# Expert matrices w1 and w3 loaded per slot tile in four chunks instead of kept in SBUF

## The reference

```python
def _L0_ffn_ref(x, gate_w, w1, w2, w3):          # 8 experts, top 2, DIM 256, HIDDEN 1024
    xt = x.reshape(-1, orig_shape[-1])
    scores = xt @ gate_w.T
    top_vals, top_idx = jax.lax.top_k(scores, TOP_K)
    top_w = jax.nn.softmax(top_vals, axis=-1)
    combine = jnp.einsum('tke,tk->te', jax.nn.one_hot(top_idx, NUM_EXPERTS, dtype=xt.dtype), top_w)
    h = jax.nn.silu(jnp.einsum('td,ehd->eth', xt, w1)) * jnp.einsum('td,ehd->eth', xt, w3)
    ye = jnp.einsum('eth,edh->etd', h, w2)
    y = jnp.einsum('te,etd->td', combine, ye)
    return y.reshape(orig_shape)
x = x + _L0_ffn_ref(_layernorm(x, axis=-1), L0_ffn_gate_w, L0_ffn_w1, L0_ffn_w2, L0_ffn_w3)
```

## Time and profile before

| | before |
|---|---|
| median of three runs | 954.2 us (951.09 to 955.96) |
| the profiled execution's own time | 948.78 us |
| its span | 947.0 us |
| mean granted TensorE clock | 0.915 of full speed |
| PE busy | 823.2 us (87%) |
| DVE busy | 630.4 us (67%) |
| ACT busy | 541.6 us (57%) |
| bytes moved by DMA | 115.83 MB |

### The profile page before, as it was taken

The page is one execution under the profiler, slowest core; times in us unless marked ns, Lnnn a source line. Parts: engine busy times, 40 slices in busy tenths (PEclk is TensorE's granted clock), DMA queues, the critical chain, the costliest instruction groups (busy, mean ns, idle before and its releaser), DMA issues.

```text
span 947.0 us, 24051 instructions
## 1 busy us (share of the span) xinstructions
PE 823.2 (87%) x9192; PEld 715.3 (76%) x9192; DVE 630.4 (67%) x941; ACT 541.6 (57%) x846; POOL 231.4 (24%) x133
## 2 busy tenths in 40 slices
PE   4888879989989998999558369999999999999994
PEld 3555558878888887888458358888888888888884
DVE  3343333636454463646334839999999999999993
ACT  2433336525443352535113129899898999898892
POOL 2244400000000000000000003455554555454542
PEclk8899989979998999989855559999999999999998
DMA  9899940000000000000807213545454545454542
GB/s 358 294 384 373 380 200 2 2 2 2 2 2 2 2 2 3 2 3 3 354 12 257 90 55 111 150 127 144 133 144 133 148 129 144 133 144 133 146 125 62
DMA packets 34661, 115.83 MB, mean 122 GB/s; under 512 B 4289, under 2 KB 15490, under 8 KB 29474
## 3 DMA queue, kind: packets, MB, share of 16 engines
q1 hardware_dynamic: 27010, 104.35, 31.4%
q0 software_dynamic: 7584, 10.49, 6.2%
HBM read 105.26 MB, written 9.57 MB: 121 GB/s over the span
## 4 chain that ended last, share of the span: by engine, by line
PE 78%; DMA 8%; DVE 6%; issue 5%; ACT 1%; SPq 1%; POOLq 0%; DVEq 0%; ACTq 0%
PE ps L428 20%; PE ps L429 19%; PE ps L430 19%; DMA ctx_t<-in_ctxT 6%; PE ps L731 3%; PE ps L614 3%; PE ps L594 2%; PE ps L602 2%; PE ps L683 1%; PE ps L668 1%; PE ps L485 1%; PE ps L507 1%; PE ps L661 1%; PE ps L694 1%; DVE den L1109 1%
## 5 line engine op out<-in xcount | busy, mean ns | idle before, releaser
L1187 DVE TENSOR_TENSOR w_lo<-w,w_hi 128x1024 fp32r<-128x1024 f32 x156 | 194.6, 1286 | 0.4 <-issue 0.4
L403 POOL DMA_INDIRECT xs_sb<-xn_d,slot_row x39 | 68.4, 1753 | 507.1 <-DVE slot_row L1307 429.9
L906 ACT ACTIVATE w_hi<-w 128x1024 fp32r x156 | 161.3, 1062 | 7.3 <-DVE tile_e L1268 7.3
L414 POOL DMA_INDIRECT out_x<-y_sb,slot_row x39 | 119.9, 3075 | 120.8 <-ACT y_sb L938 120.8
L428 PE MATMUL ps<-w_hi,xh 128*128 128x512 f32 x312 | 126.6, 406 | 1.3 <-DVE xl L1330 1.3
L430 PE MATMUL ps<-w_hi,xl 128*128 128x512 f32 x312 | 122.4, 392 | 0.0
L429 PE MATMUL ps<-w_lo,xh 128*128 128x512 f32 x312 | 122.1, 391 | 0.0
L428 PE MATMUL ps<-xT_hi,wa_hi 128*128 128x256 f32 x384 | 114.1, 297 | 2.9 <-DVE xT_lo L1085 1.5
L429 PE MATMUL ps<-xT_lo,wa_hi 128*128 128x256 f32 x384 | 110.3, 287 | 0.3 <-issue 0.3
L430 PE MATMUL ps<-xT_hi,wa_lo 128*128 128x256 f32 x384 | 110.1, 287 | 0.0
L917 ACT ACTIVATE w_hi<-w_sb 128x1024 fp32r<-128x1024 f32 x78 | 82.6, 1062 | 33.0 <-DMA w_sb<-in_w 24.6
(11 more groups left out here) (180 smaller groups left out, 1720.8 us busy)
## 6 DMA issues: line engine op xcount, KB each, us to landing
w_sb<-in_w SPq DMA_DIRECT2D x78, 512.0 KB, 4.7
ctx_t<-in_ctxT SPq DMA_DIRECT2D x16, 1028.0 KB, 7.7
ctx_n<-in_ctxN SPq DMA_DIRECT2D x16, 1024.0 KB
w<-in_w SPq DMA_DIRECT2D x8, 2048.0 KB, 11.9
stage<-in_w_a SPq DMA_DIRECT2D x16, 256.0 KB, 5.6
x_all<-in_x SPq DMA_DIRECT2D x4, 512.0 KB, 6.5
out_x<-x_all SPq DMA_DIRECT2D x1, 2048.0 KB, 13.1
xn_d<-xn SPq DMA_DIRECT2D x4, 512.0 KB, 3.9
```

What stands on the lines that cost most here:

```text
L403: pool.indirect_dma_start(xs_sb[:, :], None, xn_d, bass.IndirectOffsetOnAxis(slot_row[:, t:t + 1], 0)).then_inc(f_xs, 16)
L414: pool.indirect_dma_start(out, bass.IndirectOffsetOnAxis(slot_row[:, t:t + 1], 0), y_sb[:, :], None, compute_op=ALU.add).then_inc(f_st, 16)
L906: act.activation(w_hi[:, c, :].rearrange("p (c n) -> p c n", c=DC), w13[:, bass.ds(e, 1), c % 2, :, c // 2 * 512:(c // 2 + 1) * 512].rearr ...
L1187: dve.tensor_tensor(w_lo[:, c, :].rearrange("p (c n) -> p c n", c=DC), w13[:, bass.ds(e, 1), c % 2, :, c // 2 * 512:(c // 2 + 1) * 512].re ...
```

## The change

w13 and its loads disappear. A single buffer w13_sb of four chunks takes their place, and SP loads the four chunks of a tile's expert for every slot tile, with load_w13 standing before load_w2 in SP's loop. Chunk c of tile t waits until up_lo(t-1, c) has read the one before. up_hi waits for its chunk's semaphore f_w13[c], and ACT and DVE no longer read the expert's index. The host lays w13 out so that each chunk is contiguous within a partition's row.

```diff
-    w13 = nc.alloc_sbuf_tensor_at("w13", [P, E, 2, DC, HID], F32, offset=W13_AT)
+    w13_sb = nc.alloc_sbuf_tensor_at("w13_sb", [P, 4, PC], F32, offset=LATE_AT + EXP_BYTES)
-    l_w13 = sem("l_w13")
+    f_w13 = [sem(f"f_w13_{c}") for c in range(4)]
@@ SP
-        def load_expert(e):
-            sp.dma_start(w13[:, e, :, :, :].rearrange("p w c h -> p (w c h)"), a["w13"][e, :, :]).then_inc(l_w13, 16)
-
-        for e in range(EARLY):
-            load_expert(e)
-        sp.wait_ge(a_v, 4 * NT // 2)
-        for e in range(E // 2, E):
-            load_expert(e)
-        sp.wait_ge(a_num, NT // 2)
-        sp.wait_ge(a_y, NT // 2)
-        for e in range(EARLY + 1, E // 2):
-            load_expert(e)
-
         sp.wait_ge(a_x2, NT // 2)
...
         sp.wait_ge(g_keep, 16 * XQ)
-        sp.wait_ge(g_tr, NT)
-        load_expert(EARLY)
-
+
+        def load_w13(t):
+            e = sp.value_load(tile_e[0:1, bass.ds(t, 1)], min_val=0, max_val=E - 1)
+            for c in range(4):
+                wait(sp, f_ulo, 4 * (t - 1) + c + 1)
+                sp.dma_start(w13_sb[:, c, :], a["w13"][bass.ds(e, 1), :, c * PC:(c + 1) * PC].rearrange("e p n -> (e p) n")).then_inc(f_w13[c], 16)
...
+        sp.wait_ge(r_map, 1)
+        sp.wait_ge(a_y, NT // 2)
+        load_w13(0)
         sp.wait_ge(r_done, 1)
         load_w2(0)
         with sp.Fori(1, SLOT_TILES) as t:
+            load_w13(t)
             load_w2(t)
@@ ACT
-        def up_hi(t, cs, e):
+        def up_hi(t, cs):
             if not valid(t, SLOT_TILES):
                 return
             for c in cs:
+                wait(act, f_w13[c], 16 * (t + 1))
                 wait(act, f_up, 4 * (t - 1) + c + 1)
-                act.activation(w_hi[:, c, :].rearrange("p (c n) -> p c n", c=DC),
-                               w13[:, bass.ds(e, 1), c % 2, :, c // 2 * 512:(c // 2 + 1) * 512].rearrange("p a c n -> p (a c) n"),
-                               ACT.Copy).then_inc(f_uhi, 1)
+                act.activation(w_hi[:, c, :], w13_sb[:, c, :], ACT.Copy).then_inc(f_uhi, 1)
...
         act.wait_ge(r_map, 1)
-        act.wait_ge(l_w13, 16 * E)
-        up_hi(0, range(4), expert(0))
+        up_hi(0, range(4))
@@ DVE
-                dve.tensor_tensor(w_lo[:, c, :].rearrange("p (c n) -> p c n", c=DC),
-                                  w13[:, bass.ds(e, 1), c % 2, :, c // 2 * 512:(c // 2 + 1) * 512].rearrange("p a c n -> p (a c) n"),
-                                  w_hi[:, c, :].bitcast(F32).rearrange("p (c n) -> p c n", c=DC), ALU.subtract).then_inc(f_ulo, 1)
+                dve.tensor_tensor(w_lo[:, c, :], w13_sb[:, c, :], w_hi[:, c, :].bitcast(F32), ALU.subtract).then_inc(f_ulo, 1)
@@ host
-        "w13": np.stack([w1, w3], axis=1).reshape(E, 2, HID, DC, P).transpose(0, 4, 1, 3, 2).reshape(E, P, 2 * DC * HID),
+        "w13": np.stack([w1, w3], axis=1).reshape(E, 2, 2, HID // 2, DC, P).transpose(0, 5, 2, 1, 4, 3).reshape(E, P, 2 * DC * HID),
```

More of the change, by code:

```diff
@@ L944, in h_hi @@
             act.activation(hh[:, :, :], ps[:, 4:6, :].rearrange("p a (c d) -> p (a c) d", c=4), ACT.Copy).then_inc(f_hh, 1)
-        def expert(t):
-            return act.value_load(tile_e[0:1, bass.ds(t, 1)], min_val=0, max_val=E - 1) if valid(t, SLOT_TILES) else None
         def fstep(t):
-            e = expert(t + 1)
             silu(t, 0)
-            up_hi(t + 1, (0, 1), e)
+            up_hi(t + 1, (0, 1))
             silu(t, 1)
-            up_hi(t + 1, (2,), e)
+            up_hi(t + 1, (2,))
             x_hi(t + 1)
-            up_hi(t + 1, (3,), e)
+            up_hi(t + 1, (3,))
             down_hi(t)
@@ L1179, in _, with up_lo @@
             astep(r, r % 2)
-        def up_lo(t, cs, e):
+        def up_lo(t, cs):
             if not valid(t, SLOT_TILES):
@@ L1186, in up_lo @@
                 wait(dve, f_uhi, 4 * t + c + 1)
-                dve.tensor_tensor(w_lo[:, c, :].rearrange("p (c n) -> p c n", c=DC),
-                                  w13[:, bass.ds(e, 1), c % 2, :, c // 2 * 512:(c // 2 + 1) * 512].rearrange("p a c n -> p (a c) n"),
-                                  w_hi[:, c, :].bitcast(F32).rearrange("p (c n) -> p c n", c=DC), ALU.subtract).then_inc(f_ulo, 1)
-        def expert(t):
-            return dve.value_load(tile_e[0:1, bass.ds(t, 1)], min_val=0, max_val=E - 1) if valid(t, SLOT_TILES) else None
+                dve.tensor_tensor(w_lo[:, c, :], w13_sb[:, c, :], w_hi[:, c, :].bitcast(F32), ALU.subtract).then_inc(f_ulo, 1)
         variance(2, a_bn)
@@ L1300, in _ @@
                               ALU.is_equal).then_inc(r_in, 1)
-        up_lo(0, range(4), expert(0))
+        up_lo(0, range(4))
         dve.wait_ge(r_tab, TOP * NT // 4)
@@ L1340, in fstep @@
         def fstep(t):
-            e = expert(t + 1)
             times(t, 0)
-            up_lo(t + 1, (0, 1), e)
+            up_lo(t + 1, (0, 1))
             times(t, 1)
-            up_lo(t + 1, (2,), e)
+            up_lo(t + 1, (2,))
             x_lo(t + 1)
-            up_lo(t + 1, (3,), e)
+            up_lo(t + 1, (3,))
             down_lo(t)
```

## The result

The changed kernel took 1248.65 us (median of 4 runs, 1246.51 to 1256.3) against 955.08 us (median of 4, 951.09 to 962.39) for the kernel before. The ratio is 1.308, 95% interval 1.298 to 1.317. The profiled execution took 1249.55 us, its span is 1247.7 us. The forecast was 1189 us, in a range of 1125 to 1258.

The account below looks back on a forecast made before the run. The prediction took DVE, filling 9.47 us a slot tile, as the bound. 37 rounds at 15.8 us instead, plus 1 us, add 235 to the profiled 948.8: 1184, so 1189 us forecast, range 1125 to 1258.

Parts of the forecast that it names:

- The mechanism: Expert stage: down_lo releases SP's requests, loads land, ACT copies, DVE subtracts, next down_lo; this circle sets the tile time.
- Rival (c): Expert stage: w13 loads stay hidden if SP sends them before w2; tile 9.47 us, time 954 us; chance 5%.
- The size of a tile: Steady slot tile of the expert stage: 15.8 us against 9.47 before, low end 13.9, high end 17.8.
- five more chunks, gather and scatter: Behind w2's first half: five chunks in line at 1.35 us, 6.75 us, plus 1.2 us for gather and scatter.
- last landing to down_lo: End of the circle: one ACT copy, the last chunk's DVE subtraction and two hand-overs, 2.4 us.
- the only row of two such chunks in line: 1.35: First tile's two 512 KB chunks, landing after 4.1 and 4.9 us, gave the cost per chunk in line.
- a last landing not about 6 to 8 us behind the first: Sign in the profile after, for a tile's chunk landings, that would show the forecast wrong.
- the upper bound of 1.68 us a chunk: Chunk cost from SP's queue over 580 to 900 us, used for the tile's high end of 17.8 us.
- The last link: Circle's end: last w13 chunk lands, then up_hi(t+2, 3), up_lo(t+2, 3) and down_lo(t+1) follow.
- Rival (a): Expert stage: PE's clock falls to 1.2 GHz and PE becomes the bound; 18.9 us a tile, 1304 us; chance 8%.
- Rival (b): Expert stage: requests run ahead and DMA engines are the bound; 11.5 us a tile, 1029 us; chance 7%.
- No gain ahead of the expert stage: Dropping the eight old expert loads before the expert stage was priced at 0, as they delayed nothing.

Follow-up runs that it names:

- e1_order: Changed kernel with SP requesting w13(t+1) ahead of w2(t), same buffer and transfers: 958.94 us, ratio 1.004 to the kernel before.
- e2_double: Changed kernel with a second buffer for w13 alone, order of SP's requests kept: 1252.97 us, ratio 1.315 to the kernel before.
- e7_group: Changed kernel with all six requests of a tile waiting for the end of down_lo, w13's four before w2's two: 1184.65 us.
- e3_noscatter: Changed kernel without the scatter, and the waits for it, from the second tile on: 1234.43 us.
- e8_two: Changed kernel loading chunks 2 and 3 of w13 for the first tile only, all tiles multiplying with those: 1245.41 us.
- e6_mm2: Changed kernel with mm3 in up and down replaced by a helper of two matmuls, product lo x hi left out: 1261.4 us.
- e5_ahead: Changed kernel with two buffers for w13 and tile t+2's w13 requested behind w2(t): 953.89 us, ratio 0.999 to the kernel before.
- e9_fill2: Changed kernel with two more 512 KB loads a tile, read by nobody, behind w13's four: 1255.09 us, ratio 1.313 to the kernel before.
- e10_fill4: Changed kernel with four more 512 KB loads a tile, read by nobody, behind w13's four: 1244.98 us.
- e4_regs: Changed kernel with both reads of the expert's index ahead of the waits for down_lo, request order kept: 1272.48 us, ratio 1.329 to the kernel before.

## Why the prediction came out as it did

**The mechanism was right.** The requests for w13 stand behind w2's second half on SP, ACT waits for them and DVE for ACT. e1_order removes the loss by the order alone, e2_double shows that the buffer is not it, and e7_group puts 226 us on one wait. Rival (c) was decided by exactly the condition named: sent before w2, the loads are hidden, 954 us forecast for it and 958.94 measured.

**The size of a tile was 1.7 us short.** By the forecast's own terms, in the tile shown:

| term | forecast | measured |
|---|---|---|
| start of down_lo to SP's first request | 1.45 | 1.39 (765.94 to 767.33) |
| first landing | 4.0 | 4.1 |
| five more chunks, gather and scatter | 6.75 + 1.2 | 9.2 (771.43 to 780.66) |
| last landing to down_lo | 2.4 | 2.6 (780.66 to 783.29) |
| sum | 15.8 | 17.35; mean of all 17.49 |

37 x (17.49 - 15.8) = 63 us. The first tile's down_lo came at 573.88 instead of 571.83, 1 us more than forecast, and what follows the last round took 2 us more. 1184 + 63 + 1 + 2 = 1250 us, the profiled execution's 1249.55. The step that was mis-sized is "the only row of two such chunks in line: 1.35": it came from the first tile, where PE, ACT and DVE stood still and the two were alone. The steady row was in my hands: in the earlier trace rows the second half landed 5.5 us after its request, 2.7 us behind the first. I charged that to the scatter, and e3_noscatter shows that the scatter has some 0.3 us of it. The prediction named its own sign of this: a last landing not about 6 to 8 us behind the first would be wrong, and it came 9.2 us behind. That the total stayed in the range is due to the upper bound of 1.68 us a chunk, not to the 1.35. A small misreading beside it had no effect: the requests leave some 0.6 us apart, not 0.45, since the row of 0.89 us holds the second request's own length too; they are still faster than the landings.

**The last link was the wrong one, and right by chance.** I let the last chunk close the circle. e8_two leaves the last two out and the tile stays. What closes it is w13's second chunk, at ACT's start 11.9 us behind down_lo, and behind it 5.43 us without idle time on DVE: a copy, the second up_lo, times, the third, x_lo, the fourth. In the changed kernel both links end almost together: the last landing, 780.66, plus the forecast's 2.4 is 783.06, and down_lo starts at 783.29. So the sum hid it. With my own transfers the right link would have given 1.45 + 4.0 + 3 x 1.35 + 1.2 + 5.4 = 16.1 us.

**Rival (a), the clock.** The clock does fall, as its text said: in the changed kernel it is 0.50 from 763 to 769 of the tile shown, after PE had stopped, and the mean over the run is 0.822. It costs nothing, since PE's lost time lies in its own idle time; e6_mm2 took a third of mm3's matmuls away and the time did not fall.

**Rival (b), bandwidth.** A tile would have been 11.5 us. The engines carry more: 9.47 us a tile in e1_order. "DMA: Bandwidth & Descriptors", section Bandwidth, of the Trainium skill puts the HBM side at about 358 GB/s for loads; the steady 356 and 358 GB/s of e1_order and e5_ahead lie at that figure. But that is also what the tiles ask for: 139 GB/s before, and four chunks of 0.524 MB more in 9.47 us, 221 GB/s, make 360. Since DVE sets the beat there, these runs do not show whether more would have gone through, and single rows of the changed kernel reach 422, so it is no ceiling here. The same section lists 425 GB/s for a load of 16 MB on one core whose neighbour is idle, so the page does not rule out the prediction's stretch of 425; what the neighbour did here no run shows.

**The rest held.** No gain ahead of the expert stage; w13(0) landed in time (ACT's fourth copy starts at 540.74, DVE came to up_lo(0) at 547.17). The bytes rose by 65.0 MB.

**Open.** Why the second and third landing behind down_lo are slow. In the changed kernel not the scatter's packets (e3_noscatter), not the number of matmuls nor a running PE alone (e6_mm2), not w2's rows alone (e7_group), not the long idle time before (e9_fill2, e10_fill4). The gap between the requests is not it either: without it the second landing came later (e4_regs). That the DMA engines stand at 0.37 with five requests outstanding suggests that the time goes ahead of them, between the request and the packets; no run shows where. e1_order has weak rows too (221 GB/s at 705 to 706), but there DVE does not wait for them. A single request of 2 MB in place of four was not tried.

## What to carry to other kernels

A queue that waits in program order is part of every buffer's release: before counting bytes or buffers, write down what stands ahead of the request, and ask whether that wait comes later than the buffer's own. Here swapping two calls in SP's loop was worth 290 us, while a second buffer was worth nothing and 67% more traffic cost nothing. Price a landing from a row in the steady state, not from the quiet start of a stage, and look for the first chunk that has a full queue of work behind it, not only for the last to land.

## What the runs showed of the hardware

- The DMA engines carry six chunks of 512 KB, a gather and a scatter every 9.47 us (1.02 busy, 358 GB/s) while PE, DVE and ACT run at the pace they had at 139 GB/s.
- Of six loads requested in a burst (the changed kernel, e4_regs, e7_group), the second landed 2.0 to 4.3 us after the first, the third 1.9 to 2.1 us after the second, and the later ones 1.1 to 1.7 us apart. With the requests closer together (e4_regs) the second landed later, and the kernel was 1.6% slower than the changed one, by their ratios to the kernel before.
- From one request to the next SP needed 0.58 us with nothing between them (e4_regs, 776.37 to 776.95), and 1.53 us with a read of an index from SBUF and the loop's return between them (the changed kernel, 768.46 to 769.99).
